# Two steps of lead instead of four, six units in the first group, a last group summed by VectorE, and split LoRA operands in the setup

## The reference

```
x = x + L0_ffn(L0_cond(x))       # L0_cond: per sample a 64x64 matrix, picked by an id, mixes the channels
                                 # L0_ffn:  y @ (W + sum_n scale_n * B_n @ A_n).T + bias      (1024 -> 1024, LoRA of rank 16 x 8)
x = x + L1_ffn(L1_cond(x))       # L1_cond: per sample one of 8 adapters of rank 16, A @ (B @ x)
                                 # L1_ffn:  (silu(v @ Wg.T) * (v @ Wu.T)) @ Wd.T, hidden size 2752
Wg = NF4[gate_codes] * gate_scales   # int32 codes 0..15, one scale per block of 64; Wu and Wd likewise
```

## Time and profile before

| | us |
|---|---|
| median of 3 runs | 1083.69 (1082.5 to 1085.04) |
| the profiled execution | 1084.9 |
| its span, first to last instruction | 1083.2 |
| TensorE busy in the span | 1018.1 (94%) |
| VectorE busy | 821.6 (76%) |
| ScalarE busy | 808.4 (75%) |
| GpSimd busy | 233.9 (22%) |
| mean granted TensorE clock | 0.99 |

### The profile page before, as it was taken

How to read it: one execution, slowest core, us unless ns; L and a number is a source line. 1 busy time by engine, 2 the same in 40 slices (tenths; PEclk the granted TensorE clock), 3 DMA queues, 4 the chain that set the end, 5 groups by cost and what they waited for, 6 DMA issues and landing times.

```text
span 1083.2 us, 14501 instructions
## 1 busy us (share of the span) xinstructions
PE 1018.1 (94%) x5352; PEld 856.9 (79%) x5352; DVE 821.6 (76%) x815; ACT 808.4 (75%) x961; POOL 233.9 (22%) x285
## 2 busy tenths in 40 slices
PE   4899999999999889889999999999999999999995
PEld 3698888798888667678888888888788878888884
DVE  2788898998898878888888878878888878861220
ACT  4677787777877778889888888888888778862341
POOL 4013332442341221112111111111111011112111
PEclk9899999999999999999999999999999999999997
DMA  9735346347333326556555655655455556545667
GB/s 240 230 97 141 85 111 160 80 97 180 80 83 95 62 61 115 114 101 131 88 104 103 117 89 106 115 100 93 90 105 105 101 95 114 84 72 77 103 112 116
DMA packets 62950, 117.89 MB, mean 109 GB/s; under 512 B 6272, under 2 KB 38544, under 8 KB 62880
## 3 DMA queue, kind: packets, MB, share of 16 engines
q0 software_dynamic: 17504, 59.80, 35.3%
q1 hardware_dynamic: 44048, 56.11, 17.9%
q10 hardware_dynamic: 1328, 1.05, 0.3%
HBM read 58.22 MB, written 67.11 MB: 116 GB/s over the span
## 4 chain that ended last, share of the span: by engine, by line
PE 59%; DVE 21%; ACT 11%; issue 7%; DMA 1%; DVEq 0%; POOL 0%; SPq 0%; ACTq 0%
PE ps_z L1014 19%; PE ps_y L1014 19%; DVE val L699 12%; PE ps_gu L996 10%; ACT ring L530 7%; DVE val L701 5%; PE ps_t L933 3%; PE ps_t L925 3%; PE ps_z L891 2%; DMA w_stage<-in_L_ffn_W 1%; ACT y_hi L576 1%; DVE xs L758 1%; DVE val L718 1%; PE ps_z L871 1%; ACT inter L634 1%
## 5 line engine op out<-in xcount | busy, mean ns | idle before, releaser
L530 ACT ACTIVATE ring<-codes 128x1024 f32<-128x1024 int32 x455 | 454.6, 1052 | 114.5 <-DVE val L699 112.5
L699 DVE TENSOR_TENSOR val<-val,ring 128x1024 f32<-128x1024 f32 x260 | 320.0, 1231 | 16.5 <-ACT val L526 0.5
L701 DVE SCALAR_TENSOR_TENSOR val<-ring,val 128x1024 f32<-128x1024 f32 x195 | 240.4, 1233 | 8.6 <-DVE val L701 0.5
L502 POOL DMA_DIRECT2D out<-staged x96 | 82.6, 864 | 401.2 <-ACT staged L648 392.6
L824 DVE TENSOR_TENSOR inter<-ps_gu,inter 128x512 f32<-128x512 f32 x88 | 60.8, 691 | 142.2 <-ACT inter L634 142.1
L891 PE MATMUL ps_z<-we_hi,y_hi 128*128 128x512 f32 x256 | 106.5, 416 | 8.1 <-DVE y_lo L751 8.0
L891 PE MATMUL ps_z<-we_hi,y_lo 128*128 128x512 f32 x256 | 101.3, 396 | 0.0
L891 PE MATMUL ps_z<-we_lo,y_hi 128*128 128x512 f32 x256 | 101.0, 395 | 0.0
L634 ACT ACTIVATE inter<-ps_gu 128x512 f32<-128x512 f32 x88 | 51.7, 588 | 52.3 <-PE ps_gu L996 51.1
L444 POOL TENSOR_TENSOR st_hi<-ga_f,one 128x128 fp32r<-128x128 f32 x42 | 38.1, 908 | 226.2 <-ACT ga_f L570 206.0
L640 ACT ACTIVATE in_hi<-inter 128x512 fp32r<-128x512 f32 x88 | 55.5, 631 | 38.2 <-DVE inter L824 38.2
(11 more groups left out here) (117 smaller groups left out, 1843.9 us busy)
## 6 DMA issues: line engine op xcount, KB each, us to landing
out<-staged POOLq DMA_DIRECT2D x96, 512.0 KB, 5.4
codes<-in_L_ffn_gate_codes SPq DMA_DIRECT2D x21, 512.0 KB, 3.6
codes<-in_L_ffn_up_codes SPq DMA_DIRECT2D x21, 512.0 KB, 3.9
codes<-in_L_ffn_down_codes SPq DMA_DIRECT2D x21, 512.0 KB, 3.9
xs<-in_x SPq DMA_DIRECT2D x16, 512.0 KB, 4.1
out<-in_L_ffn_bias SPq DMA_DIRECT2D x4, 2048.0 KB, 13.3
out<-xs POOLq DMA_DIRECT2D x16, 512.0 KB, 5.5
w_stage<-in_L_ffn_W SPq DMA_DIRECT2D x8, 512.0 KB, 9.6
```

The source lines that it names most:

```text
L502: pool.dma_start(out_rows[t * P:(t + 1) * P, :], staged[:, place, :], accum_op=ALU.add).then_inc(acc_out[place], 16)
L530: act.activation(ring[:, (k - 1) % RING, :], codes[:, n % 2, :], ACT.Identity, bias=offset, scale=slope).then_inc(lines, 1)
L699: ins = dve.tensor_tensor(v, v, line, pick)
L701: ins = dve.scalar_tensor_tensor(out=v, in0=line, scalar=add, in1=v, op0=ALU.add, op1=pick)
```

## The change

Four parts.

1. `LEAD` is 2 instead of 4, in the whole kernel after the setup.
2. Group 0 has six units instead of seven, and group 4 eight instead of seven; the order within the groups follows.
3. In the last group ScalarE no longer evicts and GpSimd no longer accumulates. SyncE reads the rows of the output back into the ring (`read_back`), up to four tiles ahead and only after the last merge of all units; VectorE adds the PSUM to them (`sum_out_rows`), and SyncE stores them (`store_sum`). The last slot is computed one half of the columns after the other, and its halves are added and stored one by one.
4. In the setup the LoRA operands are split in high and low fp32r parts (`la_hi`, `la_lo`, `lbt_hi`, `lbt_lo`, in `bx_hi` and `bx_lo`), and the LoRA product is three passes of those. VectorE starts as soon as lora_B and the weights of the adapters have come. The first two pieces of W are loaded ahead of the first codes. The y of tile 0 is evicted ahead of piece 7 of W, and the second part of `ffn_z` alone waits for that piece. The wait ahead of the third load of x goes.

```
-        [("d", 3), ("d", 4), ("d", 5), ("d", 6), ("g", 12), ("u", 12), ("g", 13)],
-        [("d", 7), ("u", 13), ("d", 8), ("g", 14), ("d", 9), ("u", 14), ("d", 10), ("g", 15)],
...
-        [("d", 19), ("u", 19), ("d", 20), ("g", 20), ("d", TAIL), ("u", 20), ("t", TAIL)],
+        [("d", 3), ("d", 4), ("d", 5), ("d", 6), ("g", 12), ("u", 12)],
+        [("d", 7), ("g", 13), ("d", 8), ("u", 13), ("d", 9), ("g", 14), ("d", 10), ("u", 14)],
...
+        [("g", 19), ("d", 19), ("u", 19), ("g", 20), ("u", 20), ("d", 20), ("t", TAIL), ("d", TAIL)],
-    SPANS = [14, 16, 16, 15, 13, 0]
+    SPANS = [14, 16, 16, 15, 15, 0]
+    LAST = NT * (NG - 1)
-    LEAD = 4
+    LEAD = 2
...
+            load_w(0)
+            load_w(1)
             load_codes(0)
-            for jc in range(3):
-                load_w(jc)
+            load_w(2)
...
+            def read_back(t):
+                place, before = t % RING, LAST + t - NT
+                if t == 0:
+                    sp.wait_ge(combo, COMBOS * NU)
+                if t >= RING:
+                    sp.wait_ge(sum_out[place], 16 * (t // RING))
+                sp.wait_ge(acc_out[before % OS], 16 * (before // OS + 1))
+                sp.dma_start(ring[:, place, :], out_rows[t * P:(t + 1) * P, :]).then_inc(back_in[place], 16)
...
+            for t in range(RING - 1):
+                read_back(t)
+            for t in range(NT):
+                store_sum(t)
+                if t + RING - 1 < NT:
+                    read_back(t + RING - 1)
...
+            act.wait_ge(lora_a_in, 16)
+            act.activation(la_hi, la[:, :], ACT.Copy).then_inc(la_hi_ready, 1)
             act.wait_ge(setup_t, 1)
-            act.activation(lbt.rearrange("j (p q) -> j q p", q=DC),
+            act.activation(lbt_hi.rearrange("j (p q) -> j q p", q=DC),
...
+                if jc == DC - 1:
+                    evac_y(0, 0)
+                    evac_y(0, 1)
                 evac_w(jc)
...
-                    if slot:
+                    if 0 < slot <= LAST:
                         evac_out(slot - 1)
...
+            dve.tensor_tensor(la_lo, la[:, :], la_hi.bitcast(F32), ALU.subtract).then_inc(lora_lo_ready, 1)
+            dve.wait_ge(setup_evac, 1)
+            dve.tensor_tensor(lbt_lo.rearrange("j (p q) -> j q p", q=DC),
...
+            def sum_out_rows(t, h=None):
+                cols = slice(0, D) if h is None else slice(h * HALF, (h + 1) * HALF)
+                dve.wait_ge(down_mm, LAST + t + 1 + (h or 0))
+                dve.wait_ge(back_in[t % RING], 16 * (t // RING + 1))
+                dve.tensor_tensor(ring[:, t % RING, cols], ps_o[t % 2][:, cols], ring[:, t % RING, cols], ALU.add
+                                  ).then_inc(out_sum, 1)
...
+                    if slot > LAST:
+                        sum_out_rows(slot - 1 - LAST)
                     some_steps(at + 1, steps - 1)
...
-                    ins = pe.matmul(ps_w[jc % 2][:, h * HALF:(h + 1) * HALF], la[:, jc * P:(jc + 1) * P],
-                                    lbt[:, h * HALF:(h + 1) * HALF], start=False, stop=True)
+                    for p, (a, b) in enumerate(((la_hi, lbt_hi), (la_hi, lbt_lo), (la_lo, lbt_hi))):
+                        ins = pe.matmul(ps_w[jc % 2][:, half], a[:, jc * P:(jc + 1) * P], b[:, half],
+                                        start=False, stop=p == 2)
...
+                if part == 1:
+                    pe.wait_ge(we_lo_ready, DC)
...
-            pe.wait_ge(setup_evac, 1)
+            pe.wait_ge(lora_lo_ready, 2)
...
-            pe.wait_ge(we_lo_ready, DC)
+            pe.wait_ge(we_lo_ready, DC - 1)
...
+                if slot >= LAST + 2:
+                    pe.wait_ge(out_evac, LAST)
+                    pe.wait_ge(out_sum, slot - 1 - LAST)
```

More of the change, by code:

```diff
@@ L200, in adaln_ffn @@
         lb = wt.rearrange("p (n q) r -> p n (q r)", n=NAD)
-        lbt = xs[:, XS - 1, :]
+        lbt_hi, la_hi = bx_hi[:, 0:D], bx_hi[:, D:2 * D]
+        lbt_lo, la_lo = bx_lo[:, 0:D], bx_lo[:, D:2 * D]
         ad_araw = x1t[:, :, :]
@@ L220, in adaln_ffn @@
         ad_ids_in = sem("ad_ids_in")
-        lora_in = sem("lora_in")
+        lora_a_in = sem("lora_a_in")
+        lora_b_in = sem("lora_b_in")
         ad_b_in = sem("ad_b_in")
@@ L233, in adaln_ffn @@
         acc_out = [sem(f"acc_out{k}") for k in range(OS)]
+        back_in = [sem(f"back_in{k}") for k in range(RING)]
+        sum_out = [sem(f"sum_out{k}") for k in range(RING)]
         consts_ready = sem("consts_ready")
@@ L242, in adaln_ffn @@
         lb_scaled = sem("lb_scaled")
+        la_hi_ready = sem("la_hi_ready")
+        lora_lo_ready = sem("lora_lo_ready")
         setup_t = sem("setup_t")
@@ L281, in adaln_ffn @@
         out_evac = sem("out_evac")
+        out_sum = sem("out_sum")
         def wait(eng, semaphore, count):
@@ L401, in _, with store_sum @@
                 load_codes(n)
+            def read_back(t):
[6 more added lines that the diff above has]
+                sp.dma_start(ring[:, place, :], out_rows[t * P:(t + 1) * P, :]).then_inc(back_in[place], 16)
+            def store_sum(t):
+                if t == NT - 1:
+                    for h in range(2):
+                        sp.wait_ge(out_sum, t + h + 1)
+                        sp.dma_start(out_rows[t * P:(t + 1) * P, h * HALF:(h + 1) * HALF],
+                                     ring[:, t % RING, h * HALF:(h + 1) * HALF]).then_inc(sum_out[t % RING], 16)
+                else:
+                    sp.wait_ge(out_sum, t + 1)
+                    sp.dma_start(out_rows[t * P:(t + 1) * P, :], ring[:, t % RING, :]).then_inc(sum_out[t % RING], 16)
+            for t in range(RING - 1):
[4 more added lines that the diff above has]
+                    read_back(t + RING - 1)
+            for place in range(RING):
+                tiles = range(place, NT, RING)
+                sp.wait_ge(sum_out[place], 16 * (len(tiles) + (NT - 1 in tiles)))
         @block.gpsimd
@@ L503, in accumulate @@
                                ).then_inc(acc_out[place], 16)
-            for slot in range(NT * NG):
+            for slot in range(LAST + 1):
                 if is_gu(TURN_AT.get(slot - 1)):
@@ L509, in _ @@
                     accumulate(slot - 1)
-            accumulate(NT * NG - 1)
             for place in range(OS):
-                pool.wait_ge(acc_out[place], 16 * len(range(place, NT * NG, OS)))
+                pool.wait_ge(acc_out[place], 16 * len(range(place, LAST, OS)))
         @block.scalar
         def _(act):
-            act.dma_start(lb, lora_b.rearrange("n (p q) r -> p n (q r)", p=P)).then_inc(lora_in, 16)
-            act.dma_start(lw[:, :], lora_w.partition_broadcast(P)).then_inc(lora_in, 16)
-            act.dma_start(la[:, :], lora_a.rearrange("n r d -> (n r) d")).then_inc(lora_in, 16)
+            act.dma_start(lb, lora_b.rearrange("n (p q) r -> p n (q r)", p=P)).then_inc(lora_b_in, 16)
+            act.dma_start(lw[:, :], lora_w.partition_broadcast(P)).then_inc(lora_b_in, 16)
+            act.dma_start(la[:, :], lora_a.rearrange("n r d -> (n r) d")).then_inc(lora_a_in, 16)
             def line(n, k):
@@ L778, in _ @@
                 at += 1
+                if jc == DC - 1:
+                    low_y(0, 0)
+                    low_y(0, 1)
                 low_w(jc)
@@ L858, in _ @@
             assert at >= STEPS * NU
+            sum_out_rows(NT - 1, 0)
+            sum_out_rows(NT - 1, 1)
         @block.tensor
@@ L997, in gate_up, with down @@
                 ins.then_inc(gu_mm, 1)
-            def down(g, t, ks):
+            def down(g, t, ks, halves=(0, 1)):
                 b, s, last = t // TPB, t % TPB, len(GROUPS[g]) - 1
                 slot = NT * g + t
-                if slot >= 2:
+                if slot >= LAST + 2:
+                    pe.wait_ge(out_evac, LAST)
+                    pe.wait_ge(out_sum, slot - 1 - LAST)
+                elif slot >= 2:
                     pe.wait_ge(out_evac, slot - 1)
@@ L1012, in down @@
                     for p, (v, w) in enumerate(passes):
-                        for h in range(2):
+                        for h in halves:
                             ins = pe.matmul(ps_o[slot % 2][:, h * HALF:(h + 1) * HALF],
@@ L1031, in _ @@
                     before, now = TURN_AT.get(slot - 1), TURN_AT.get(slot)
+                    if slot == NT * NG - 1:
+                        for h in range(2):
+                            down(g, t, range(chunks), (h,))
+                        continue
                     down(g, t, range(chunks - 1))
```

24 lines of the change are left out of this document (9 added, 15 removed), and 4 rows, old and new, of the table BY_GROUP.

## The result

The changed kernel takes 1037.45 us (median of 4 runs, 1036.96 to 1037.77) against 1083.45 us before; the ratio is 0.957, 95% interval 0.956 to 0.959. The forecast was 1050 us, range 1038 to 1063: right in its sign, too small by a quarter (46.0 us won, 34 forecast), and outside the range by half a microsecond. The rival "all waits go", with 1037 us, names the time. In phase A it names the mechanism too; that its sum hits is partly luck, since it has 2.5 us too much for the setup and 3.5 each for group 0 and for the first gate and up products, and too little for phase A (17.6 against 22.0), the end and groups 1 to 4.

What follows compares the result with a forecast made beforehand. TensorE sets the pace in group 1 but waits in setup, phase A and group 0, where ScalarE's queued lines wait for VectorE. Terms from setup to end sum to 34.0 us won, from 1083.69 to 1050 us, range 1038 to 1063.

Steps and rivals of the forecast that it cites:

- all waits go: Rival: the waits in setup, phase A and group 0 vanish at their upper bounds, giving 1037 us; chance 0.10.
- start of `ffn_z`: Setup: cheaper LoRA products let the first `ffn_z` start at 40.5 us, 5.6 us won (3 to 7.5).
- low clock at the start: First 24 matmuls of phase A: with the gap gone they take 5.5 instead of 8.42 us, 2.9 us won.
- waits of phase A: Phase A: the shorter lead wins 11 us of 17.6 us of TensorE's waits, bounds 5 and 17.6.
- around the first gate and up products: After phase A: TensorE loses some 4 us there to the same cause; 1.5 us won, 0 to 3.
- group 0, without the moved unit: Group 0: shorter lead and one unit less cut TensorE's waits, 7.6 us won, bounds 3 and 10.6.
- groups 1 to 4, without it: Groups 1 to 4: new waits where groups take more units, 0.5 us lost, 0 to 5.
- last group: Last group: VectorE's sum ends after TensorE wants the bank again, 0.7 us three times, 2.2 us lost (0 to 6).
- end: After the last matmul: 13.3 us shrink to 5.2, 8.1 us won, or 2.2 if the silence belongs to any program.
- silent end: Last 5 to 6 us without activity, taken as GpSimd's and gone; the rival that it stays: 1056 us, chance 0.12.
- strided low part: Setup: VectorE writing `lbt_lo` at about twice a plain pass would delay the first LoRA product 1.2 us, gain 4.4 us.
- VectorE starves: Rival: in phase A VectorE lacks a line twice per tile, 1.05 us each, 33.6 us lost, 1103 us; chance 0.06.

Runs made afterwards that it cites:

- extra_vector: Changed kernel with two more unused VectorE passes of 384 columns in each tile of phase A: 1051.65 us.
- extra_half: Changed kernel with one more unused VectorE pass of 384 columns in each tile of phase A: 1042.05 us.
- lead2_alone: Kernel before with ScalarE's lines two steps ahead instead of four, nothing else changed: 1056.69 us.
- rotate_lead4: Kernel before, still four steps ahead, with the five ring buffers taken in turn over all lines of all units: 1052.70 us.
- units_alone: Kernel before with six units in group 0 and eight in group 4, nothing else changed: 1079.67 us.
- last_alone: Kernel before with the last group summed by VectorE and stored by SyncE, nothing else changed: 1074.89 us.
- no_setup: Changed kernel with the old setup, keeping the lead of two, new units and new last group: 1042.59 us.
- after_lead4: Changed kernel with a lead of four again: 1071.55 us.
- pool_end: Changed kernel with one wait for VectorE's last sum added at the end of GpSimd's list: 1040.38 us.
- after_rotate4: Changed kernel with the ring buffers taken in turn over all lines and a lead of four: 1035.51 us.

## Why the prediction was wrong, point by point

| step | forecast, us | measured, us |
|---|---|---|
| start of `ffn_z` | 5.6 | 5.0 (46.07 to 41.11) |
| low clock at the start (24 matmuls, start to next start) | 2.9 | 2.7 (8.24 to 5.56) |
| waits of phase A | 11 | 22.0 |
| around the first gate and up products | 1.5 | -0.5 |
| group 0, without the moved unit | 7.6 | 7.1 |
| groups 1 to 4, without it | -0.5 | 3.3 |
| last group | -2.2 | -1.9 |
| end | 8.1 | 10.1 |

The measured terms are differences of stage lengths, 47.8 in all, against 47.7 between the spans. The mechanisms were right: ScalarE held up by its own lines, the gap with its low clock, VectorE's sum behind `in_lo`, GpSimd as the owner of the silent end. What failed was above all one size.

**The waits of phase A**: the step that takes 11 us of TensorE's 17.6 us of waits as won. Two errors lie in it, both to the same side.

The first, 6.6 us. The prediction gave VectorE 20.1 us a tile, 19.5 of work and 0.6 of waits that stay, put this beside TensorE's 20.3 in a tile with two units and 18.1 in a tile with one, and left waits for the latter. By work alone the two bounds are level: TensorE needs 11 x 20.3 + 5 x 18.1 = 313.8 us, and VectorE 16 x 19.5 = 312. Measured is 313.2. Two steps of the working each leave waits, and neither held. With the 0.6 us on top VectorE would need 16 x 20.1 = 321.6 us. Without it, but with no slack going over from tile to tile, the five tiles with one unit would still cost 5 x 1.4 = 7 us. The worry itself was right: `extra_vector` and `extra_half` show only 4 to 5 us of room in the whole phase, which puts VectorE, its waits included, at about 309 us or 19.3 a tile (an estimate from A less this room).

The second, 4.4 us, is a bound that was set too low. 17.6 us was the profile's idle time of those waits, and as idle time it was all won: 19.7 to 2.1. A wait costs more than its idle time. TensorE's recorded busy time fell by 7.2 us with the same matmuls, of which 2.7 are the low clock, and the other 4.5 go with 17 waits, about 0.26 us each. The timeline before shows such a restart:

```profile
214.82 0.39 PE L891 MATMUL ps_z<-we_hi,y_lo 128*128 128x512 f32 x1
216.49 2.05 PE L933 MATMUL ps_gu<-wt,ad_at 128*128 128x128 f32 x16 [1.28 <-ACT wt L542]
218.30 0.47 PE L891 MATMUL ps_z<-we_hi,y_hi 128*128 128x512 f32 x1
```

From the start of the last matmul to that of the next after the product it is 3.48 us. At the pace without a wait it is 0.23 + 1.70, the 1.70 being this product elsewhere (237.43 to 239.13 before the change). The loss is 1.55 for an idle time of 1.28.

**The low clock** is not tied to the start of phase A. With the old setup and the same wait of 3.58 us it came there in three traces (the kernel before, `lead2_alone`, `rotate_lead4`) and did not in three (`units_alone`, `last_alone`, `no_setup`); in `last_alone` it came at 370 us instead, behind a wait of 2.4 us for `x1t`. The prediction's "0 if some other gap brings the same clock" was a fair bound.

**Around the first gate and up products** the forecast took the same cause and was wrong. The wait for `wd_early_lo` is there in both kernels and grows, from 0.6 to 1.6 us. VectorE's sum and low part of that unit stand behind the steps that it still has to do at the end of the phase.

**Groups 1 to 4** won 3.3 us instead of losing 0.5, by the same cause as phase A: with a lead of four again they take 2.7 us more (`after_lead4`, 497.7 against 495.0), and the buffers in turn alone save 4.1 of 495.7 us in the kernel before (`rotate_lead4`). **Group 0** came out as forecast, 7.1 for 7.6.

**The last group** cost 1.9 for 2.2. In its place the prediction read 0.7 us where its rows give 1055.8 - 1055.27 = 0.5.

**The end**: the silent part went, as assumed, and the last stores of 256 KB landed 2.0 us after their issue rather than the 3.5 us of the load of that size.

**The setup** came out near the forecast, 5.0 for 5.6, but only in company of the short lead (or the buffers in turn), which the prediction did not see. The third piece of W did not begin an us earlier, as the prediction had it, but at the same 24.02; 3.3 of the 5.0 us are the wait ahead of `ffn_z` and the rest the shorter pieces. Of the strided low part it had taken ScalarE's price as the nearest row:

```profile
16.56 2.02 DVE L812 TENSOR_TENSOR bx_lo<-ps_t,bx_hi 128x1024 fp32r<-128x1024 f32 x1 [0.69 <-ACT bx_hi L628]
```

It took 2.02 us against 1.23 for the plain subtraction, 0.8 more and not the 1.2 of a doubled pass. That agrees with the rule of the Trainium skill, page "SBUF — State Buffer", section "Door 1: The DMA port swizzle (why `[64,N]` ≈ `[32,N]`)", for VectorE too. The forecast gain of the setup did not shrink to 4.4 us by it; what the write costs behind the third piece was not tried.

**The rival "VectorE starves"** was given 1.05 us twice per tile at a lead of two. Measured are 3.8 us in all of phase A; at a lead of one it exists, in the groups, as a loop and not as a sum of small waits.

## What to carry to other kernels

Where engines walk fixed lists, look for the queued instruction with the least slack, here two of eight lines whose buffer was read only four places back. Everything behind it inherits its wait, and the buffers taken in turn over all units removed it without memory and without touching the lead. Bound what freed waits are worth by the sums of work of each engine over the whole phase, not tile by tile, and add the restart of each wait to the idle time that the profile shows. A reordering can depend on another part of the same change: the setup was worth 1.2 us alone and some 5 us in company. Where a stretch grows, look at the granted clock before calling it a wait: the 2 us that "next" grew in `extra_half` were clock.

## What the runs showed of the hardware

- GpSimd needs some 6 us to close its list at the end of a program, with or without an open DMA of its own (13.3 and 7.1 us from the last matmul to the end; 6.4 us from the last thing it waited for in `pool_end`); a kernel whose last work is on SyncE ended after 3.2 us.
- A wait of TensorE costs about 0.26 us more than the idle time shown (4.5 us of recorded busy time over 17 waits).
- After 3.6 us without work on TensorE the first 24 matmuls of 512 columns took 8.24 instead of 5.56 us in the kernel before, with the granted clock at its lower level, 1.2 GHz. The same wait left them at full pace in `units_alone`, `last_alone` and `no_setup`, and waits of 2.3 to 2.7 us brought the lower level in `after_rotate4`, `last_alone` and group 0 of the kernel before. The length of a single gap does not decide it.
- A VectorE pass over 1024 columns of fp32 that writes elements 32 bytes apart took 2.02 us, a contiguous one 1.23.
